# Narrower adjacency words, look-ups behind the maxima and smaller first parts in a two-layer graph kernel

## What is computed

```python
q = (x[sub] @ Wq.T + bq).reshape(-1, 8, 64); k = (x[obj] @ Wk.T + bk).reshape(-1, 8, 64)
att = (q * k).sum(-1) / 8
scores = zeros(8, n, n).at[:, sub, obj].set(att)      # pairs that are edges get a score
scores = where(adj == 0, -inf, scores); diagonal = 1e-7
x = layernorm(x + (softmax(scores).sum(0) / 8) @ x)
x = layernorm(x + adj @ (x @ W1) + b1)
```

## Time and profile before

| what | value |
|---|---|
| median of 3 runs | 176.11 us (175.93 to 176.72) |
| the profiled execution | 176.58 us, its span 174.8 us |
| TensorE busy | 164.5 us of the span, 94% |
| VectorE, ScalarE, GpSimd busy | 122.4, 73.5, 71.1 us |
| mean granted clock of TensorE | 0.994 |
| bytes moved | 22.65 MB, 130 GB/s over the span |

### The profile page before, as it was taken

One profiled execution on the slowest core, in us unless ns is written; L12 is line 12 of the kernel. 1 busy time (PEld: TensorE's weight loads), 2 busy tenths in 40 slices (PEclk: granted clock), 3 DMA queues, 4 the chain that ended last, 5 costly groups with the idle time before them and its releaser, 6 DMA issues.

```text
span 174.8 us, 2906 instructions
## 1 busy us (share of the span) xinstructions
PE 164.5 (94%) x1054; PEld 88.1 (50%) x1054; DVE 122.4 (70%) x365; ACT 73.5 (42%) x124; POOL 71.1 (41%) x91
## 2 busy tenths in 40 slices
PE   3999999999999999979999999999999989999960
PEld 3964545565564445434445457545664434444440
DVE  2886689998978997594935866498972167657481
ACT  6867639769523333195041116142122004232441
POOL 7787777777777775248821704000000000000000
PEclk9999999999999999999999999999999999999997
DMA  5999889995299411030000530000000001311233
GB/s 133 392 368 307 323 274 363 393 387 218 77 338 325 167 60 60 4 63 0 0 1 4 159 101 6 0 2 0 4 0 0 7 6 67 117 60 73 84 120 120
DMA packets 12999, 22.65 MB, mean 130 GB/s; under 512 B 4478, under 2 KB 5662, under 8 KB 12850
## 3 DMA queue, kind: packets, MB, share of 16 engines
q1 hardware_dynamic: 7570, 18.17, 29.5%
q10 hardware_dynamic: 3280, 3.07, 5.1%
q0 software_dynamic: 2128, 1.16, 3.1%
HBM read 16.70 MB, written 5.68 MB: 128 GB/s over the span
## 4 chain that ended last, share of the span: by engine, by line
PE 90%; DVE 5%; POOL 1%; issue 1%; ACT 1%; DVEq 0%; POOLq 0%
PE acc L1250 27%; PE acc L1183 22%; PE acc L1329 12%; PE tr L1183 8%; PE tr L1169 4%; PE tr L1164 4%; PE tr L1329 3%; PE acc L1353 2%; PE tr L1287 2%; PE tr L1319 2%; PE tr L1197 1%; DVE st L832 1%; PE tr L1308 1%; PE tr L1304 1%; DVE last_st L1144 0%
## 5 line engine op out<-in xcount | busy, mean ns | idle before, releaser
L594 POOL DMA_INDIRECT ed_adj<-in_adj,ed_idx x47 | 48.5, 1032 | 14.5 <-issue 14.0
L1250 PE MATMUL acc<-adjT,x1s 128*128 128x512 f16 (+3 forms) x264 | 52.5, 354 | 0.9 <-DVE x1s L895 0.9
L1183 PE MATMUL acc<-xs,adjT 128*128 128x512 f16 (+1 forms) x176 | 40.1, 379 | 0.0
L1250 PEld LDWEIGHTS acc<-adjT,x1s 128*128 128x128 f16 (+1 forms) x264 | 24.9, 98 | 25.4 <-DVE x1s L895 1.4
L1183 PEld LDWEIGHTS acc<-xs,adjT 128*128 128x128 f16 (+1 forms) x176 | 16.8, 98 | 18.7
L1329 PE MATMUL acc<-whl,xs 128*128 128x512 f16 (+1 forms) x108 | 23.8, 370 | 0.0
L1329 PEld LDWEIGHTS acc<-whl,xs 128*128 128x128 f16 x108 | 10.6, 98 | 11.8
L1183 PE MATMUL tr<-xs,adjT 128*128 128x512 f16 (+1 forms) x66 | 15.2, 379 | 0.0
L686 ACT ACTIVATE xs<-acc 128x512 f16<-128x512 f32 (+1 forms) x12 | 6.4, 540 | 20.7 <-PE acc L1250 20.7
L638 ACT CAST adjT<-stage 128x1408 f16<-128x1408 f32 x9 | 12.3, 1361 | 3.6 <-DMA stage<-in_adj_T 3.3
L602 POOL DMA_INDIRECT found<-in_adj,top_i x8 | 10.6, 1320 | 6.3 <-DVE top_i L922 4.1
(11 more groups left out here) (250 smaller groups left out, 221.4 us busy)
## 6 DMA issues: line engine op xcount, KB each, us to landing
stage<-in_adj_T SPq DMA_DIRECT2D x9, 704.0 KB, 7.1
x_sb<-in_x SPq DMA_DIRECT2D x3, 768.0 KB, 6.3
sums_dram<-y ACTq DMA_DIRECT2D x6, 256.0 KB, 3.3
sums_dram<-xd ACTq DMA_DIRECT2D x5, 256.0 KB, 4.5
out<-y SPq DMA_DIRECT2D x5, 256.0 KB, 2.0
stage<-in_adj_T SPq DMA_DIRECT2D x3, 384.0 KB, 5.8
hot<-row_dram SPq DMA_DIRECT2D x1, 1024.0 KB, 9.8
stage<-in_L_gnn_weight SPq DMA_DIRECT2D x1, 1024.0 KB, 5.6
```

What stands on the lines that cost most here:

```text
L594: nc.gpsimd.indirect_dma_start(out=ed_adj[0:EP, c:c + 1], out_offset=None, in_=adj_flat, in_offset=bass.IndirectOffsetOnAxis(ap=ed_idx[0:E ...
L1183: last = mm(sum_bank(i)[:, :], adjT[0:width[k], k, i * P:(i + 1) * P], xs[0:width[k], half, k, :], start=(k == 0 and half == 0), stop=(k = ...
L1250: ins = mm(mix_bank(u)[:, 0:j - i], x1s[0:width[k], half, k, f * P:(f + 1) * P], adjT[0:width[k], k, i:j], start=(k == 0 and half == 0), s ...
```

## The change

- Words of 22 bits: `bit_eye` has 64 columns and a column of ones. Rows 64 to 127 of a block go to the same columns as rows 0 to 63, times 2^11 (`fold_eye`); all is scaled by 2^-6 and scaled back in `fold`, which no longer removes the diagonal. `table` is put together from the lower and upper 11 bits.
- Maxima behind the exact look-ups: `left_candidates` takes the eight largest keys of the 32 filtered columns alone, and GpSimd looks these up behind its 47, without waiting for them to land. `top_candidates` comes after the look-ups, with the 47 exact ones and the eight found, and its maxima need no further look-up. The count of too many candidates has two parts (`left_over`, `many_candidates`), with a semaphore of its own, `many_ready`, on which TensorE waits before compaction.
- FIRST_PARTS are 2, 3, 3 and 3 key tiles; 48 warming products; tile 2 is loaded, cast and used in two parts.
- The pairs are loaded from ScalarE's queue, first; row and column numbers are stored behind loads 3 and 4; `split_left` comes after two tiles of `split_x`.
- Mixing units 0 and 1 take turns per key tile; `low_x1` of tile 9 comes before `left_candidates`; the selects of tile 10 come one part sooner; numbering and compaction stand one row of mixing closer.

The diff, cut to its core:

```diff
+WP = P // 2
+WORD_ONE = 2.0 ** -6
...
-FIRST_PARTS = ((0, 3), (3, 6), (6, 9), (9, T))
-WORDS_BEFORE = {2: (2,), 3: (3,), 4: (4,), 5: (5, 6), 6: (7, 8), 7: (9, 10)}
+FIRST_PARTS = ((0, 2), (2, 5), (5, 8), (8, T))
+THIRD_PARTS = ((0, 6), (6, T))
+WORDS_BEFORE = {3: (3,), 4: (4,), 5: (5, 6), 6: (7, 8), 7: (9, 10)}
+FOLDS_AT = {2: (2,), **WORDS_BEFORE}
...
-MIX_ORDER = [(u, k) for u in range(2) for k in range(T - 1)] + [(u, T - 1) for u in range(2)] + [(u, k) for u in range(2, 12) for k in range(T)]
+MIX_ORDER = [(u, k) for k in range(T - 1) for u in range(2)] + [(u, T - 1) for u in range(2)] + [(u, k) for u in range(2, 12) for k in range(T)]
...
-        co = sb("co", [P, 8, T])
-        two_c0, neg_c0, gain, inv, eps_row, diag_bit, power, aii_all = (co[:, n, :] for n in range(8))
+        co = sb("co", [P, 6, T])
+        two_c0, neg_c0, gain, inv, eps_row, aii_all = (co[:, n, :] for n in range(6))
...
-        bit_eye = sb("bit_eye", [P, T, P + 1], f16)
-        folded = sb("folded", [P, P], i16)
-        fold_in = sb("fold_in", [P, 2, P], i16)
+        bit_eye = sb("bit_eye", [P, T, WP + 1], f16)
+        fold_eye = sb("fold_eye", [P, WP], f16)
+        folded = sb("folded", [P, WP], i32)
+        fold_in = sb("fold_in", [P, 2, WP], i32)
...
-        ident16 = sb("ident16", [P, P], f16)
...
-            sp.dma_start(ed_i[:], pairs.rearrange("(p c) two -> p c two", p=EP)).then_inc(edges_loaded, 16)
...
-            sp.dma_start(x_sb[:, T - 2, :], rows(x, T - 2)).then_inc(x_loaded[3], 16)
+            sp.dma_start(x_sb[:, 8:T - 1, :], x[8 * P:(T - 1) * P, :].rearrange("(t p) h -> p t h", p=P)).then_inc(x_loaded[3], 16)
...
-            load_adj(2)
+            for n, (a, b) in enumerate(THIRD_PARTS):
+                sp.dma_start(stage[:, 2, a * P:b * P], adj_t[2][:, a * P:b * P]).then_inc(third_loaded[n], 16)
+            load_adj(3)
+            load_adj(4)
...
-            load_adj(3)
-            load_adj(4)
...
-            nc.gpsimd.affine_select(out=ident16[:], in_=ones16[:], compare_op=ALU.is_equal, fill=0.0,
-                                    base=0, pattern=[[-1, P]], channel_multiplier=1).then_inc(consts, 1)
-            for k in range(T):
-                nc.gpsimd.memset(power[:, k:k + 1], float(2 ** k)).then_inc(consts, 1)
-            nc.gpsimd.memset(bit_eye[:, :, P:P + 1], 1.0).then_inc(consts, 1)
+            nc.gpsimd.affine_select(out=fold_eye[:], in_=ones16[:, 0:WP], compare_op=ALU.is_equal, fill=0.0,
+                                    base=0, pattern=[[-1, WP]], channel_multiplier=1).then_inc(pool_step, 1)
+            pool.wait_ge(pool_step, 4)
+            nc.gpsimd.affine_select(out=fold_eye[:], in_=fold_eye[:], compare_op=ALU.not_equal, fill=float(2 ** T),
+                                    base=-WP, pattern=[[-1, WP]], channel_multiplier=1).then_inc(consts, 1)
+            nc.gpsimd.memset(bit_eye[:, :, WP:WP + 1], 1.0).then_inc(consts, 1)
...
-            pool.wait_ge(edges_looked_up, 16 * LOOKED)
-            nc.gpsimd.memset(stackL[0:64, :], 1.0).then_inc(ones_laid, 1)
-
...
+            pool.wait_ge(edges_looked_up, 16 * LOOKED)
+            pool.wait_ge(top_found, 16 * TOP)
+            nc.gpsimd.memset(stackL[0:64, :], 1.0).then_inc(ones_laid, 1)
...
-                act.wait_ge(adj_loaded[t % RING], 16 * (t // RING + (t % RING == 2)))
+                act.wait_ge(adj_loaded[t % RING], 16 * (t // RING))
...
+            act.dma_start(ed_i[:], pairs.rearrange("(p c) two -> p c two", p=EP)).then_inc(edges_loaded, 16)
+            act.dma_start(aii_all, adj_diag).then_inc(diag_loaded, 16)
...
-            act.dma_start(aii_all, adj_diag).then_inc(diag_loaded, 16)
...
-                nc.scalar.mul(bit_eye[:, k, 0:P], ident16[:], float(2 ** k)).then_inc(bit_eye_ready, 1)
+                nc.scalar.mul(bit_eye[:, k, 0:WP], fold_eye[:], WORD_ONE * 2 ** k).then_inc(bit_eye_ready, 1)
...
-            cast_adj(2)
+            for n, (a, b) in enumerate(THIRD_PARTS):
+                act.wait_ge(third_loaded[n], 16)
+                ins = nc.scalar.copy(adjT[:, a:b, 2 * P:3 * P], stage[:, 2, a * P:b * P].rearrange("p (k i) -> p k i", i=P))
+                ins.then_inc(third_cast if n == 0 else adj_cast, 1)
...
-                V.tensor_copy(counts[:, i, 0:1], bank[:, P:P + 1]).then_inc(dve_step, 1)
-                (V.scalar_tensor_tensor(folded[:] if i == 0 else new, ident16[:], diag_bit[:, i:i + 1], bank[:, 0:P], ALU.mult, ALU.add)
-                 ).then_inc(words_folded, 1)
+                V.tensor_copy(counts[:, i, 0:1], bank[:, WP:WP + 1]).then_inc(dve_step, 1)
+                V.tensor_scalar(folded[:] if i == 0 else new, bank[:, 0:WP], 1.0 / WORD_ONE, None, ALU.mult).then_inc(words_folded, 1)
...
-            dve.wait_ge(consts, 4 + T)
+            dve.wait_ge(consts, 4)
...
-            step(V.scalar_tensor_tensor(diag_bit, aii_all, -1.0, power, ALU.mult, ALU.mult))
-            split_left()
...
+                if t == 1:
+                    split_left()
...
-            best, ti, got = top_key[0:EP], top_i[0:EP], found[0:EP]
+            best, ti, got = top_key[0:EP, 0:TOP], top_i[0:EP], found[0:EP]
+
+            left_cand = cand[:, LOOKED:EC]
+            left_key, left_i8 = top_key[0:EP, TOP:2 * TOP], top_i[0:EP, 0:3]
...
-                step(V.scalar_tensor_tensor(cand[:, LOOKED:EC], word, 0.0, ekey[:, LOOKED:EC], ALU.is_gt, ALU.mult))
+                step(V.scalar_tensor_tensor(left_cand, word, 0.0, ekey[:, LOOKED:EC], ALU.is_gt, ALU.mult))
+                step(V.max(left_key, left_cand))
+                step(V.tensor_copy(left_i8[:, 0], left_key))
+                step(V.tensor_scalar(left_i8[:, 1], left_i8[:, 0], 11, None, ALU.logical_shift_right))
+                step(V.tensor_scalar(left_i8[:, 2], left_i8[:, 0], 2047, None, ALU.bitwise_and))
+                step(V.scalar_tensor_tensor(pos[0:EP, 0], left_i8[:, 1], float(N), left_i8[:, 2], ALU.mult, ALU.add))
+                V.tensor_scalar(ti[:, 3], pos[0:EP, 0], -1.0, 0.0, ALU.add, ALU.max).then_inc(top_ready, 1)
+
+            def left_over():
+
+                step(V.scalar_tensor_tensor(ed_junk[0:EP, LOOKED:EC], left_cand, 0.0, ones[0:EP, 0:LEFT], ALU.is_gt, ALU.mult, accum_out=many[0:EP]))
+                step(V.tensor_scalar(many[0:EP], many[0:EP], float(TOP), FAR, ALU.is_gt, ALU.mult))
...
-                step(V.scalar_tensor_tensor(cand[:, 0:LOOKED], ed_adj[0:EP], 1.0, ekey[:, 0:LOOKED], ALU.is_equal, ALU.mult))
-                step(V.max(best, cand))
+                V.scalar_tensor_tensor(cand[:, 0:LOOKED], ed_adj[0:EP], 1.0, ekey[:, 0:LOOKED], ALU.is_equal, ALU.mult).then_inc(dve_step, 1)
+                steps += 1
+                dve.wait_ge(top_found, 16 * TOP)
+                step(V.scalar_tensor_tensor(cand[:, LOOKED:LOOKED + TOP], got, 1.0, left_key, ALU.is_equal, ALU.mult))
+                step(V.max(best, cand[:, 0:LOOKED + TOP]))
+                V.tensor_scalar(flag[0:EP], best, 0.0, None, ALU.is_gt).then_inc(flags_ready, 1)
...
-                step(V.scalar_tensor_tensor(pos[0:EP, 0], ti[:, 1], float(N), ti[:, 2], ALU.mult, ALU.add))
-                V.tensor_scalar(ti[:, 3], pos[0:EP, 0], -1.0, 0.0, ALU.add, ALU.max).then_inc(top_ready, 1)
+
+            def many_candidates():
+
+                step(V.scalar_tensor_tensor(ed_junk[0:EP, 0:LOOKED + TOP], cand[:, 0:LOOKED + TOP], 0.0, ones[0:EP, 0:LOOKED + TOP],
+                                            ALU.is_gt, ALU.mult, accum_out=some[0:EP]))
+                V.tensor_scalar(many16[0:EP], some[0:EP], many[0:EP], float(TOP), ALU.add, ALU.is_gt).then_inc(many_ready, 1)
...
+                    low_x1(T - 2)
...
-                for t in WORDS_BEFORE.get(i + 1, ()):
+                for t in FOLDS_AT.get(i + 1, ()):
...
-                    V.tensor_copy(table[:], folded[:]).then_inc(table_ready, 1)
-                if i + 1 in WORDS_BEFORE:
-                    coefs(WORDS_BEFORE[i + 1])
+                    V.tensor_scalar(fold_in[:, 0, :], folded[:], 2 ** T - 1, None, ALU.bitwise_and).then_inc(dve_step, 1)
+                    V.tensor_scalar(fold_in[:, 1, :], folded[:], T, None, ALU.logical_shift_right).then_inc(dve_step, 1)
+                    steps += 2
+                    dve.wait_ge(dve_step, steps)
+                    V.tensor_copy(table[:], fold_in[:, :, :].rearrange("p a w -> p (a w)")).then_inc(table_ready, 1)
+                if i + 1 in FOLDS_AT:
+                    coefs(FOLDS_AT[i + 1])
...
-                if i == T - 1:
-                    top_candidates()
...
-                if i >= 1:
+                if 1 <= i < T - 1:
...
-            step(V.scalar_tensor_tensor(ed_junk[0:EP], cand, 0.0, ones[0:EP, 0:EC], ALU.is_gt, ALU.mult, accum_out=many[0:EP]))
-            step(V.tensor_scalar(many16[0:EP], many[0:EP], float(TOP), None, ALU.is_gt))
-            step(V.tensor_scalar(pos[0:EP, 2], best, 0.0, None, ALU.is_gt))
+            left_over()
...
-            dve.wait_ge(top_found, 16 * TOP)
```

(22 more changed lines are left out.)

31 lines of the change are left out of this document (17 added, 14 removed).

## The result

The changed kernel takes 173.96 us (median of 4 runs, 173.92 to 174.09), the one before 176.07 us beside it (4 runs, 175.93 to 176.72): a ratio of 0.986, with a 95% interval of 0.981 to 0.991. It is faster by 2.1 us, where 5.6 were forecast. Its profiled execution took 173.95 us with a span of 172.2. Ratios here leave out runs that lie over 1.5% above the fastest of their kernel, medians and ranges do not, and the profiles of e1_pairs_sync and e2_parts_3332 are of such runs.

A forecast was written before the change was run, and what follows sets the result against it. TensorE, busy 94% of the span, was taken to bound the kernel. Terms of 2.0 + 2.9 + 0.9 - 0.2 = 5.6 us took the median from 176.11 to 170.5 us, with a range of 169.4 to 172.4.

The forecast's parts named there:

- Part 1: Start: with 48 warming products and smaller first parts, tile 2 begins at 18.65, not 20.69: 2.0 us gained.
- Rival (a): Start gives less: x lands as late as now or the clock rises later; 0.8 us instead of 2.0, 171.7; chance 0.14.
- Part 2: Words products of tiles 2 to 10: 65 columns instead of 129, 30 ns instead of 59 each; 2.9 us gained.
- Part 3: Start of mixing: tile 9's x1s ahead of the candidates and units in turns remove TensorE's wait; 0.9 us gained.
- Part 4: Numbering after the maxima's look-ups: flags in time with 0.8 us to spare, many_ready late; 0.2 us lost.
- Part 5: Middle of the first stage: VectorE's folds and the cast of tile 8 fit by less than 1 us; 0.
- Rival (d): Middle: the cast of tile 8 or 10, or a fold, comes too late; 1.3 us lost, 171.8; chance 0.07.
- Standing to the median: Whole kernel: the profiled execution lay 0.47 us above the median of 176.11, so 171.0 became a median of 170.5.

The follow-up runs named there:

- e1_pairs_sync: Changed kernel with the pairs loaded first on SyncE's queue again: 174.84 us, 0.991 of the kernel before.
- e2_parts_3332: Changed kernel with first parts of 3, 3, 3 and 2 key tiles again: 173.53 us, 0.984 of the kernel before.
- e13_best: Changed kernel with parts 3, 3, 3, 2, split_left after six tiles, column numbers' broadcast behind load 10, count's product behind compaction: 172.33 us, 0.977 of before.
- e13_again: The same kernel as e13_best, run once more: 171.37 us, 0.971 of the kernel before.
- e14_parts_split_late: Changed kernel with parts 3, 3, 3, 2 again and split_left after six tiles instead of two: 173.28 us, 0.984 of the kernel before.
- e15: e13_best with GpSimd's memset of stackL behind the two gathers of the slots: 171.87 us, 0.973 of the kernel before.
- e16: e15 with VectorE's second low half of the projection weights also moved behind the numbering constants: 171.50 us, 0.972 of the kernel before.
- e5_wide: Changed kernel with words products of 129 columns again, 64 of them read by nobody: 174.90 us, 0.994 of the kernel before.
- e10_cols_behind: Changed kernel with the column numbers' broadcast (0.5 MB) behind adjacency load 10 instead of ahead of load 8: 172.91 us, 0.982 of the kernel before.
- a0_again: Changed kernel, unaltered, run once more: 174.87 us, 0.990 of the kernel before.
- e11: e10_cols_behind with the row numbers' broadcast (1 MB) also moved, behind load 8: 173.57 us, 0.985 of the kernel before.
- the second profile: The kernel before, unchanged, run once more for a second profile of its start: 176.08 us, 0.999 of the kernel before.

## Why the prediction was wrong

It was wrong in size: 2.1 us came and 5.6 were forecast, and 173.96 us lie above the range's upper edge of 172.4. By its own steps:

- **Part 1, the start (2.0 us; 0.0 to 0.4 came). This is the step that failed most.** It put x's last part at 15.2 us, from one row of one profile (15.66) less the issue of the pairs. With parts of 2, 3, 3 and 3 it came at 15.48 to 17.26 us in ten profiles, median 16.55; moving the pairs brought nothing that shows (e1_pairs_sync). With 3, 3, 3 and 2 it came at 15.46 to 17.14 in eight, median 15.78. What follows x was right: where it came by 15.97, tile 2's words begin at 18.89 to 18.98 (e13_best, e13_again, e14_parts_split_late, e15, e16; not in e2_parts_3332, with its gap), near the 18.65 of the forecast; in the nine profiles with parts of 2, 3, 3, 3, narrow words and x later than 16 us they begin 3.46 to 3.48 us behind x. Rival (a) named this, at 0.8 us of gain; it was less. Whether the parts move the landing, with the same bytes ahead of it, stays open: the medians differ by 0.8 us, but each of the two sets has a profile in the other's range.
- **Part 2, the words (2.9 us; 2.67 came).** Right. Eleven products take 0.35 to 0.36 us, 32 to 33 ns each against 30 forecast, and e5_wide gets the 2.65 us back in that stretch by the width alone. The case that the step cites from the Trainium skill ("TensorE: Matmul & The Clock Gate", "Wait — 56ns, not 53.3ns?"), 62 ns a product where decoding is not done in hardware, is not what this kernel shows.
- **Part 3, x1s (0.9 us; 1.18 came).** Right in the wait; of the two reasons given the low half alone is enough. The row of the wait says 0.91 us, but the 86 products took 18.59 us without it and 19.77 with it. A wait costs more than its row says, here by 0.27 us, in the middle by 0.16 (1.19 against 1.03). Of that, 0.16 us is how the rows count: a product is shown as 0.38 us long while the next one starts 0.22 us behind it (51.79 and 52.01 in after), and the idle row begins only where the shown product ends. The other 0.1 us stays open.
- **Part 4, look-ups and count (0.2 us; 0.41 to 0.56 came).** The wait for the count was 0.41 us, twice the forecast, inside its bounds. The look-ups of the maxima began at 71.19 and not 68.95, since the maxima were late with everything before, and the flags' operation took 0.93 us beside a memset that the forecast had said was done by 86. All the room went, and in e13_best 1.2 us beyond it. The step also said that nothing moves the 47 look-ups in front: they end at 68.64 before, at 68.52 in after, and between 66.4 and 70.4 in the changed kernels. The look-up of 2.10 us that the step calls an agreement shows the stretch alone, not the mode in which VectorE's 2.29 us operation runs.
- **Part 5, the middle (0; a loss of 1.19 us came).** The step said that the cast of tile 8 would fit, since TensorE wants it at 39.7, and it did. What it left out is what stands behind that cast on ScalarE: x1 of tile 3 and the root of tile 4, on which VectorE's y of tile 5 hangs, and the picks three tiles on. Rival (d) had the right place and the right price (1.3 us) but the wrong wait. e10_cols_behind shows the cause by taking most of it away: VectorE's wait for the root goes from 1.11 us (a0_again) to nothing and TensorE's for the pick from 1.16 to 0.23. The stretch takes 17.17 us then, not 16.78: the last 0.4 us (0.1 to 0.5 in e11, e13, e15 and e16) are VectorE's own work, which the step took to be in time.
- **Standing to the median.** The 0.47 us by which the profiled execution lay above the median was carried over to the new kernel. It belonged to the start of that one execution (0.42 us there against the second profile) and went with it.

The likeliest single errors, 1.6 to 2.0 us and 1.2 us, both came of reading a transfer's time from one profile and asking only when TensorE wants it. With the old parts and `split_left` later, the order of the queue and the count's product changed, the kernel takes 172.33 us in one set of runs and 171.37 in another, 3.9 and 5.1 us below the one before on the same chip. That this is near the 5.6 us forecast for the change as it stood doesn't bear the forecast out: it took other edits to get there.

## What to carry to other kernels

When work is taken off the busy engine, each load and in-order queue that used to be in time by a little becomes the next bound: follow a late load through its cast to everything queued behind that cast, not only to the engine that reads its result. A landing time read from one profile is one draw from a spread (here 1.8 us wide), and slack on the busy engine hides it: before, x at 15.66 and at 17.14 gave the same time within 0.6 us. Take a gain and its give-back apart by differences of start times between fixed points; they add up to the span and show 1.2 us returned some 20 us after they were won. And look, in each engine's first microseconds too, for a short operation that takes five times as long as its like: beside another engine's long one it may hold up a whole chain.
